# Self-attention of a decoder layer on one Trainium2 core: values as the stationary operand, four column tiles, and two stage borders in another order

## The chip, the cores and the metric

The kernel runs on one core of one Trainium2 chip. The metric is the device time of that core in microseconds (us), the median of several runs. TensorE is called PE here (its weight loads PEld), VectorE DVE, ScalarE ACT, GpSimd POOL and SyncE, which issues all the transfers, SP.

## The reference

One decoder layer on x of 8 sequences x 128 tokens x 512 channels, float32: causal self-attention (32 heads of 16 channels, ALiBi bias), cross-attention to a context (32 query heads over 8 key/value heads of 128 channels, rotary embedding), and a feed-forward block, each followed by a residual add and a layer normalisation. The part that matters here:

```python
scores = einsum('bqhd,bkhd->bhqk', q, k) / sqrt(16) + alibi   # causal, h = 32 heads
attn = softmax(scores, axis=-1)
out = einsum('bhqk,bkhd->bqhd', attn, v).reshape(B, S, D)
x = layernorm(x + out @ w_out.T + b_out)
```

## The kernel before

Matmuls in the kernel run on "split" operands: a float32 value is written as a high part in the reduced format fp32r and a low part (value minus high part), and a product is three matmuls (high x high, high x low, low x high: `product`, L34). ACT makes the high part by a copy, DVE or POOL the low part by a subtraction.

There are four stages, each with a method for every engine, and every engine works through its own list in order, held back by semaphores alone. **A** (`ProjectSelf`) computes q, k and v of self-attention: 16 tiles of q and k, which go through DRAM into the layout of the heads, and 8 tiles of v, one for each sequence, and splits the context on the side. Each tile goes from PE to `A_val` (DVE), is split by ACT and POOL, and the values end in `vhl` (16 high, then 16 low channels for every head). **B** (`AttendSelf`) is the self-attention, 64 steps n = 8b + G: sequence b, group G of 4 heads. **C** is the cross-attention (64 steps) and **D** the feed-forward block.

In a step n of B, PE (`tensor`) issues the scores of group n (2 matmuls, L777), the product of probabilities and values of group n-4 (`weigh`, L748 and L749), the transposes of the probabilities of group n-2 (L789), then half a tile (6 matmuls) of the cross-attention's keys and values (`project`), which fill PE while the softmax is on the way. Twice in eight steps 6 matmuls of the output projection come ahead of that (`close`). DVE (`minima`, L825) adds the mask, writes the negated scores to `prob` (3 slots) and takes their minimum; ACT takes the exponentials in place with their sum (L676); the transposed probabilities are split by ACT (L659) and DVE (L833). In `weigh` the 128x128 transposed probabilities of one head are the stationary operand and the head's 32 or 16 value columns are moving, so the output has queries on partitions. ACT (L668) and DVE (L840) add the two halves, POOL divides 16 heads at a time by their sums (`scale`, L595), PE transposes the result (L797), ACT and DVE split it (L690, L845).

The cross-attention's keys and values share the engines. With four steps to a pair of tiles, n = 0 mod 4 has the last of both: ACT, behind the exponentials of step n, makes the high part of a value tile (L683) and of a key tile (L695); DVE the low part of the value tile (L895); POOL, first thing in its step n, the low part of the key tile (L615, waits for L695). POOL adds the rotated halves at n = 3 mod 4 (L627). POOL also has the low parts of the weights (L166), the inverse root (L108) and the normalisation of a row (L113).

At the border of A and B the context's last pieces and the first weights of B come through `stage`, a ring of five slots that A uses with three more of its own. A loads the pieces, then B's first five pieces, each as soon as its slot is free; B's first weight piece (`B_wk`) takes slot 0, which holds one of A's last. At the border of B and C, seven more steps (`STEPS` = 71) take the last groups through; the tables `QUERY`, `ROTATE` and `NEXT_SPLIT` spread the first four query tiles of C (`cross.project`, `cross.rotate`) over them. C's step 1 is the first that begins with `scores`, since scores(0) is issued in B.

Of the kernel before, what the change touches and what calls it, by code (L numbers as in the profile page):

```python
# [23 lines left out]
KV = 4 * NT  # L24

# [113 lines left out]
class Ring:  # L139
# [9 lines left out]

    def load(self, eng, n, src):  # L150

        wait(eng, self.s_lo, n - self.SLOTS + 1)
        dst = self.stage[:, n % self.SLOTS, :]
        if len(src.shape) == 3:
            dst = dst.rearrange("p (g n) -> p g n", g=src.shape[1])
        eng.dma_start(dst, src).then_inc(self.s_piece[n % self.SLOTS], 16)

    def hi(self, eng, n, out):

        eng.wait_ge(self.s_piece[n % self.SLOTS], 16 * (n // self.SLOTS + 1))  # L160
        eng.activation(out, self.stage[:, n % self.SLOTS, :], ACT.Copy).then_inc(self.s_hi, 1)  # L161

    def lo(self, eng, n, hi, out):

        eng.wait_ge(self.s_hi, n + 1)
        eng.tensor_tensor(out, self.stage[:, n % self.SLOTS, :], hi.bitcast(F32), ALU.subtract).then_inc(self.s_lo, 1)  # L166
# [49 lines left out]
class ProjectSelf:  # L216

    RING = 8  # L220
# [13 lines left out]
    def __init__(self, chip, stage, cT, vhl, heads, ident, power, trig, dram):  # L234
        sem = lambda name: chip.sem("A_" + name)
        self.stage, self.cT, self.vhl, self.heads, self.ident, self.power, self.trig = stage, cT, vhl, heads, ident, power, trig
# [15 lines left out]
        self.s_val, self.s_vhi, self.s_vlo = sem("val"), sem("vhi"), sem("vlo")  # L252
# [22 lines left out]
    def sync(self, eng, ring, sources):  # L275
# [28 lines left out]
        for n in range(self.CONTEXT + C, len(self.pieces)):  # L304
            self.load_piece(eng, n)
        heads.load(eng, 0, 1)
        for n in range(Ring.SLOTS):
            eng.wait_ge(self.s_lo, max(j for j in range(len(self.pieces)) if j % self.RING == n) + 1)
            ring.load(eng, n, sources[n])
# [11 lines left out]
    def scalar_tile(self, eng, i):  # L321

        kind, m, h = self.order[i]
        if kind == "qk":
            for n in self.pieces_with(i):
                self.piece_hi(eng, n)
        eng.wait_ge(self.s_val, i + 1)
        src = self.val[:, i % 2, :]
        if kind == "qk":
            if i >= self.heads.RING:  # L330
                eng.wait_ge(self.heads.s_store[i % self.heads.RING], 16 * (i // self.heads.RING))
            dst = self.tiles[i % self.heads.RING][:, 0, :]
        else:
            dst = self.vhl[:, m, :, 0:DH]
            src = src.rearrange("p (h d) -> p h d", d=DH)
        eng.activation(dst, src, ACT.Copy).then_inc(self.s_vhi, 1)
        if kind == "v":
            for n in self.pieces_with(i):
                self.piece_hi(eng, n)
# [42 lines left out]

    def vector_tile(self, eng, i):
# [6 lines left out]
        wait(eng, self.s_vlo, i - 1)  # L390
# [3 lines left out]
        if kind == "v":  # L394
            eng.tensor_tensor(out, acc, self.bv[:, :], ALU.add).then_inc(self.s_val, 1)  # L395
# [15 lines left out]
    def gpsimd_tile(self, eng, i):  # L411

        kind, m, h = self.order[i]
        eng.wait_ge(self.s_vhi, i + 1)
        src = self.val[:, i % 2, :]
        if kind == "qk":
            hi, lo = (self.tiles[i % self.heads.RING][:, j, :] for j in range(2))
        else:
            src = src.rearrange("p (h d) -> p h d", d=DH)
            hi, lo = self.vhl[:, m, :, 0:DH], self.vhl[:, m, :, DH:2 * DH]  # L420
        eng.tensor_tensor(lo, src, hi.bitcast(F32), ALU.subtract).then_inc(self.s_vlo, 1)

    def gpsimd(self, eng):
# [12 lines left out]
        for i in range(len(self.order)):  # L436
            self.gpsimd_tile(eng, i)
            if i == 0:
                eng.wait_ge(self.s_ident, 32)
                eng.tensor_scalar(self.trig[:, 0:2, :], self.trig[:, 0:2, :], -1.0, None, ALU.mult)\  # L440
                   .then_inc(heads.s_causal, 1)


class AttendSelf:

# [13 lines left out]

    NEXT_LOAD = {57: range(5), 62: (5, 6), 64: (7,), 67: (8,)}  # L460
    NEXT_SPLIT = {60: (0,), 61: (1,), 62: (2,), 65: (3,), 70: (4, 5, 6, 7)}
    QUERY = {64: 0, 65: 1, 66: 2, 67: 3}
# [460 lines left out]
class AttendCross:  # L923
# [248 lines left out]
    def vector(self, eng, n):  # L1172
# [5 lines left out]
        if n == 0:  # L1178
            self.minima(eng, n)
# [601 lines left out]
```

## Time and profile before

| what | value |
|---|---|
| median of 3 runs | 954.91 us (952.61 to 955.36) |
| the profiled execution | 952.4 us, its span 950.6 us |
| busy in the span | PE 901.9, PEld 765.9, DVE 673.7, ACT 498.4, POOL 522.3 us |
| mean granted PE clock | 0.989 of full speed |

The span runs from the first to the last instruction on the core. "Busy" of PE counts matmuls whose modelled spans overlap, so what a matmul costs is the distance to the start of the next. A view by stretches gives the busy time of each engine with the number of its instructions, and the granted clock (1.00 is 2.4 GHz, 0.50 is 1.2 GHz). A timeline row is: start, length, engine, line, instruction, tiles, shape, count, and in brackets the engine's idle time ahead of it with what ended it.

### The profile page before, as it was taken

What the parts mean: (1) busy time and instruction counts of PE and PEld (TensorE: products, weight loads), DVE (VectorE), ACT (ScalarE), POOL (GpSimd) and SP (SyncE); (2) the same over time, 40 slices, a digit from 0 to 9 for tenths busy, and PEclk for the clock granted to TensorE, in tenths of its full rate; (3) what the DMA queues carried; (4) which work ended last, traced back from release to release, by engine and by line L of the source; (5) the groups of instructions that cost most, each with busy time, mean ns of one, the idle gap of its engine ahead of it and who ended that gap; (6) DMA issues with size and microseconds to landing.
All of it is one profiled execution on the core that took longest, in us unless ns stands there. A gap on an engine that the chain in (4) does not pass through costs nothing.

```text
span 950.6 us, 15757 instructions
## 1 busy us (share of the span) xinstructions
PE 901.9 (95%) x4812; PEld 765.9 (81%) x4812; DVE 673.7 (71%) x2166; ACT 498.4 (52%) x1565; POOL 522.3 (55%) x443
## 2 busy tenths in 40 slices
PE   7996999999999789999999999999999999999996
PEld 6785988888888668888888888888888887787884
DVE  5465767777777658777777777777777777655646
ACT  4335877776777245455555455555445566340320
POOL 4544843353234566666666666666666678654001
PEclk9998999999999989999999999999999999999999
DMA  7688986576544611131131311313113113010000
GB/s 273 257 204 189 248 178 121 141 162 122 134 122 157 254 56 34 42 125 34 34 122 34 126 42 34 123 34 116 41 44 123 34 56 109 15 34 23 23 12 33
DMA packets 68371, 96.65 MB, mean 102 GB/s; under 512 B 7232, under 2 KB 44352, under 8 KB 67264
## 3 DMA queue, kind: packets, MB, share of 16 engines
q1 hardware_dynamic: 68288, 95.65, 34.7%
q8 instruction: 39, 0.64, 0.3%
q14 instruction: 44, 0.36, 0.2%
HBM read 68.33 MB, written 27.26 MB: 101 GB/s over the span
## 4 chain that ended last, share of the span: by engine, by line
PE 79%; ACT 6%; issue 6%; DVE 6%; POOL 2%; DMA 0%; POOLq 0%; ACTq 0%; DVEq 0%
PE banks L34 61%; PE banks L1102 4%; PE banks L1082 3%; PE banks L789 3%; PE banks L749 2%; ACT B_prob L676 2%; PE banks L748 2%; PE banks L1103 2%; PE banks L777 1%; POOL x L1620 1%; PE banks L121 1%; ACT C_prob L1032 1%; DVE A_val L395 1%; ACT cT L319 0%; DVE B_prob L825 0%
## 5 line engine op out<-in xcount | busy, mean ns | idle before, releaser
L34 PE MATMUL banks<-C_wo,C_o 128*128 128x512 f32 x768 | 190.3, 396 | 2.2 <-DVE C_o L1195 1.0
L34 PE MATMUL banks<-xT,C_w 128*128 128x512 f32 x768 | 186.9, 393 | 1.5 <-DVE xT L136 1.5
L34 PEld LDWEIGHTS banks<-xT,C_w 128*128 128x128 f32 x768 | 145.0, 190 | 32.0 <-issue 1.9
L34 PEld LDWEIGHTS banks<-C_wo,C_o 128*128 128x128 f32 x768 | 139.5, 188 | 30.5 <-issue 2.3
L1023 ACT ACTIVATE C_q<-C_t 128x512 fp32r<-128x512 f32 x64 | 40.5, 632 | 170.2 <-POOL C_t L1208 170.2
L676 ACT ACTIVATE B_prob<-B_prob,B_top 128x128 f32<-128x128 f32 x256 | 99.5, 391 | 33.2 <-DVE B_top L825 32.4
L1216 POOL TENSOR_TENSOR C_q<-C_t,C_q 128x512 fp32r<-128x512 f32 x64 | 82.9, 1295 | 47.6 <-ACT C_q L1023 47.6
L1032 ACT ACTIVATE C_prob<-C_prob,C_top 128x128 f32<-128x128 f32 x256 | 98.9, 389 | 0.3 <-DVE C_top L1166 0.3
L1208 POOL TENSOR_TENSOR C_t<-C_t,C_t 128x512 f32<-128x512 f32 x64 | 83.1, 1298 | 5.7 <-DVE C_t L1147 5.7
L1102 PE MATMUL banks<-C_kv,C_q 128*128 128x256 f32 x256 | 68.2, 344 | 5.0 <-issue 4.8
L166 POOL TENSOR_TENSOR C_wo<-stage,C_wo 128x512 fp32r<-128x512 f32 x32 | 41.0, 1284 | 57.8 <-ACT C_wo L161 57.8
L166 POOL TENSOR_TENSOR C_w<-stage,C_w 128x512 fp32r<-128x512 f32 x32 | 41.1, 1284 | 56.5 <-ACT C_w L161 56.5
L1224 POOL TENSOR_TENSOR C_prob<-C_prob,C_rden 128x512 f32<-128x512 f32 x64 | 66.5, 1040 | 2.2 <-DVE C_rden L1177 2.1
L825 DVE CUSTOM_DVE_ANT_0 B_prob<-banks,causal 128x128 f32<-128x128 f32 x256 | 58.9, 286 | 10.1 <-issue 9.8
L1049 ACT ACTIVATE C_o<-banks 128x512 fp32r<-128x512 f32 x64 | 38.3, 598 | 50.2 <-PE banks L34 50.2
L1195 DVE TENSOR_TENSOR C_o<-banks,C_o 128x512 fp32r<-128x512 f32 x64 | 44.2, 691 | 25.7 <-ACT C_o L1049 25.6
L1145 DVE TENSOR_TENSOR C_t<-banks,trig 128x512 f32<-128x512 f32 x64 | 44.2, 690 | 25.5 <-PE banks L34 25.5
L1166 DVE CUSTOM_DVE_ANT_0 C_prob<-banks,C_prob 128x128 f32<-128x128 f32 x256 | 58.9, 286 | 2.7
L34 PE MATMUL banks<-cT,B_wk 128*128 128x512 f32 x192 | 52.4, 409 | 7.9 <-POOL B_wk L166 7.7
L749 PE MATMUL banks<-vhl,B_pT 128*128 128x16 f32 x256 | 59.2, 256 | 0.0
L833 DVE TENSOR_TENSOR B_pT<-banks,B_pT 128x512 fp32r<-128x512 f32 x64 | 44.1, 689 | 20.4 <-ACT B_pT L659 20.2
L34 PE MATMUL banks<-C_pT,C_kv 128*128 128x512 f32 x192 | 54.3, 391 | 4.2 <-DVE C_pT L1184 2.1
(156 smaller groups left out, 2132.1 us busy)
## 6 DMA issues: line engine op xcount, KB each, us to landing
C_kv<-cross_kv_d SPq DMA_DIRECT2D x8, 2048.0 KB, 8.9
cross_kv_d<-B_k_out SPq DMA_DIRECT2D x16, 512.0 KB, 3.0
cross_kv_d<-B_v_out SPq DMA_DIRECT2D x16, 512.0 KB, 4.8
stage<-wq_dram SPq DMA_DIRECT2D x32, 256.0 KB, 2.6
stage<-wo_dram SPq DMA_DIRECT2D x32, 256.0 KB, 2.6
heads_q<-heads_q_d SPq DMA_DIRECT2D x96, 64.0 KB, 3.7
heads_k<-heads_k_d SPq DMA_DIRECT2D x96, 64.0 KB, 3.8
heads_q_d<-cT SPq DMA_DIRECT2D x8, 512.0 KB, 2.6
```

The lines of the kernel that those rows point to most:

```text
L34: mm = eng.matmul(out, stationary[i], moving[j], start=first and n == 0, stop=last and n == len(PASSES) - 1)
L166: eng.tensor_tensor(out, self.stage[:, n % self.SLOTS, :], hi.bitcast(F32), ALU.subtract).then_inc(self.s_lo, 1)
L676: last = eng.activation(e, e, ACT.Exp, bias=self.top[:, n % 4, h:h + 1], scale=-1.0, accum_out=self.total[:, HG * G + h:HG * G + h + 1])
L749: mm = eng.matmul(out[:, at:at + DH], self.pT[1][:, m % 2, h * S:(h + 1) * S], v[:, 0:DH], start=False, stop=True)
L825: last = eng.tensor_tensor_reduce(self.prob[:, n % 3, h * S:(h + 1) * S], self.sc[n % 2][:, h * S:(h + 1) * S], self.heads.causal, 1.0, 3e ...
L1032: last = eng.activation(e, e, ACT.Exp, bias=self.top[:, n % 2, h:h + 1], scale=-1.0, accum_out=self.total[:, n % 2, h:h + 1])
L1102: eng.matmul(out, q[0][:, h, tok], both, start=True, stop=False)
L1145: eng.tensor_tensor(by_batch(t1), by_batch(bank), cos, ALU.mult).then_inc(self.s_cos, 1)
L1166: last = eng.tensor_tensor_reduce(self.prob[:, n % 2, h * S:(h + 1) * S], self.sc[:, h // 2, h % 2, 0, :], self.prob[:, n % 2, h * S:(h + ...
L1208: eng.tensor_tensor(t1, t1, t2, ALU.add).then_inc(self.s_sum, 1)
L1216: eng.tensor_tensor(self.query(r, 1), by_batch(self.t1[:, r % 2, :]), self.query(r, 0).bitcast(F32), ALU.subtract).then_inc(self.s_qlo, 1)
L1224: eng.tensor_tensor(e, e, self.rden[:, (n - 1) % 2, :].unsqueeze(2).broadcast_to([P, self.Q, S]), ALU.mult).then_inc(self.s_norm, 1)
```

## The change

The values stay in full precision (`v`, float32, not split): for two heads the columns lie as v, 16 zeros, v, so that the 32 columns [v | 0] belong to the first head and [0 | v] to the second. `weigh` takes them as the stationary operand, with the transposed probabilities (float32, not split either, 128 columns) moving; two groups (8 heads) are done at once, four pairs of heads in the four column tiles of the array (output partitions 32q to 32q+31), 8 matmuls in every second step. The output is thereby already transposed, with channels on partitions. The division by the sums therefore moves ahead of the transposes, to all of the probabilities: `inverse` on DVE, `norm` on POOL, in every step. ACT's copy of the transposed probabilities stays (`copy_turned`); DVE's subtraction L833, the addition L668 and L840, `scale`, and the transposes L797 go. The row's normalisation moves from POOL to DVE, and `prob` has 4 slots. In A the value tiles are no longer split, POOL clears the zero columns, and `B_wk` takes the ring's slot that comes free first. At the end of B the last steps are written out in another order, the same in kind for all engines. In C, `scores(0)` moves to C's step 0, behind its two query tiles. Cut to its core (where a removed line is left out, it is in the functions above):

```diff
+VW = 3 * DH * HS // 2
...
+    def slot(self, n):                      # Ring
+        return (n + self.SLOTS - 1) % self.SLOTS
...
         heads.load(eng, 0, 0)               # ProjectSelf.sync
+        for n in range(Ring.SLOTS):
+            eng.wait_ge(self.s_lo, max(j for j in range(len(self.pieces)) if j % self.RING == ring.slot(n)) + 1)
+            ring.load(eng, n, sources[n])
+            if n == 0:
+                for j in range(self.CONTEXT + C, len(self.pieces)):
+                    self.load_piece(eng, j)
         heads.load(eng, 0, 1)
...
+        for n in self.pieces_with(i):       # scalar_tile
+            self.piece_hi(eng, n)
+        if i < self.QK:
+            eng.wait_ge(self.s_val, i + 1)
...
-        wait(eng, self.s_vlo, i - 1)        # vector_tile
+        wait(eng, self.s_vlo, min(i - 1, self.QK))
...
+            eng.tensor_tensor(self.values_of(self.v[:, m, 0:VW], 3)[:, :, 0:3:2, :], self.values_of(acc, 2),
+                              self.values_of(self.bv[:, :], 2), ALU.add).then_inc(self.s_val, 1)
...
+        for i in range(self.QK):            # ProjectSelf.gpsimd
             self.gpsimd_tile(eng, i)
...
+            if i == 1:
+                for b in range(B):
+                    last = eng.memset(self.values_of(self.v[:, b, 0:VW], 3)[:, :, 1, :], 0.0)
+                last.then_inc(self.s_pad, 1)
...
+    OT, CLOSE, ROW, ROOT, NORMAL, TURN, TAKE = 11, (12, 13), 14, 15, 16, 17, 18
...
+    def norm(self, eng, m):
+        eng.wait_ge(self.s_rden, m + 1)
+        e = self.prob[:, m % 4, :].rearrange("p (h s) -> p h s", h=HG)
+        eng.tensor_tensor(e, e, self.rden[:, m % 2, :].unsqueeze(2).broadcast_to([P, HG, S]), ALU.mult).then_inc(self.s_norm, 1)
...
     def gpsimd(self, eng, n):
         j = self.tile("k", n, 2)
         if j is not None:
+            self.key_lo(eng, j)
+        if n > 0:
+            self.norm(eng, n - 1)
...
+    def gpsimd_end(self, eng):
+        self.norm(eng, self.NS - 1)
+        self.key_lo(eng, len(self.FILL) // 2 - 1)
+        for i in range(3, 7):
             self.cross.piece_lo(eng, i)
...
     def scalar(self, eng, n):
+        if n >= self.LT:
+            self.copy_turned(eng, n - self.LT)
+        b = self.closing(n, self.TAKE)
         if b is not None:
             self.rows.hi(eng, b)
+        b = self.closing(n, self.OT)
+        if b is not None:
+            self.output_hi(eng, b)
+        eng.wait_ge(self.s_top, n + 1)
+        wait(eng, self.s_rden, n - 1)
...
+            self.value_hi(eng, j)
         j = self.tile("k", n, 2)
         if j is not None:
+            self.key_hi(eng, j)
...
+    def transpose(self, eng, m):
+        eng.wait_ge(self.s_norm, m + 1)
+        wait(eng, self.s_turned, m)
...
+    def weigh(self, eng, k):
+        b, c = k // C, k % C
+        eng.wait_ge(self.s_turned, 2 * k + 2)
...
+        for second in range(2):
+            for q in range(HG):
+                head = 2 * q + second
+                at = VW // HS * 2 * (4 * c + q) + DH * second
+                mm = eng.matmul(self.ov[b % 2][32 * q:32 * q + 32, c * S:(c + 1) * S], self.v[:, b, at:at + 2 * DH],
+                                self.pT[:, (2 * k + head // HG) % 4, head % HG * S:(head % HG + 1) * S],
+                                start=second == 0, stop=second == 1)
...
     def tensor(self, eng, n):
+        self.scores(eng, n)
+        if n >= self.LV and n % 2 == 0:
+            self.weigh(eng, (n - self.LV) // 2)
+        if n >= self.LT:
+            self.transpose(eng, n - self.LT)
...
+    def tensor_end(self, eng):
+        self.weigh(eng, (self.NS - self.LV) // 2)
+        self.transpose(eng, self.NS - 2)
+        self.cross.project(eng, 0)
+        self.cross.project(eng, 1, (0, 1))
+        self.transpose(eng, self.NS - 1)
+        self.turn(eng, B - 2)
+        self.cross.project(eng, 1, (2, 3))
+        self.weigh(eng, self.NS // 2 - 1)
+        self.cross.project(eng, 2, (0, 1))
+        self.close(eng, B - 1, range(C))
+        self.cross.project(eng, 2, (2, 3))
+        self.cross.project(eng, 3)
+        self.turn(eng, B - 1)
...
+    def inverse(self, eng, m):
+        eng.wait_ge(self.s_exp, m + 1)
+        wait(eng, self.s_norm, m - 1)
+        eng.reciprocal(self.rden[:, m % 2, :], self.total[:, m % 2, :]).then_inc(self.s_rden, 1)
...
     def vector(self, eng, n):
+        self.minima(eng, n)
+        if n > 0:
+            self.inverse(eng, n - 1)
...
             for n in range(c.STEPS):        # PE's list, stage C
                 d.tensor_ahead(eng, n)
+                if n < 3:
+                    c.queries(eng, n)
                 c.transpose(eng, n)
-                if n > 0:
-                    c.scores(eng, n)
+                c.scores(eng, n)
                 c.outputs(eng, n)
```

## Rows read from the trace of the kernel before

**Rows 1.** Stretches: length, busy (x) of PE, PEld, DVE, ACT, POOL; clock, DMA, GB/s.

```profile
90.00:325.00 235.00, 225.06 (x1453) 199.21 (x1452) 176.07 (x765) 173.04 (x645) 109.44 (x94) 1.00 0.67 167
75.50:83.00 7.50, 0.00 (x0) 0.00 (x0) 4.88 (x14) 2.97 (x6) 4.12 (x3) 0.76 0.69 128
83.20:86.00 2.80, 2.77 (x7) 2.25 (x8) 0.00 (x0) 2.34 (x10) 0.90 (x1) 0.50 0.95 249
325.96:330.75 4.79, 0.00 (x1) 0.03 (x1) 1.89 (x5) 0.76 (x2) 3.84 (x4) 0.77 0.16 68
```

**Rows 2.** PE's timeline, one step of B, and the same place eight steps later.

```profile
265.03 0.40 PE L777 MATMUL banks<-heads_k,heads_q 128*128 128x256 f32 x2
265.26 0.18 PE L748 MATMUL banks<-vhl,B_pT 128*128 128x32 f32 x1
...
266.08 0.66 PE L789 MATMUL banks<-ident,B_prob 128*128 128x128 f32 x4
266.49 1.63 PE L34 MATMUL banks<-cT,B_wk 128*128 128x512 f32 x6
267.95 0.40 PE L777 MATMUL banks<-heads_k,heads_q 128*128 128x256 f32 x2
...
293.81 0.40 PE L777 MATMUL banks<-heads_k,heads_q 128*128 128x256 f32 x2
```

**Rows 3.** Groups of instructions in 90:325, by shape: busy us, mean ns, idle before.

```profile
L748 PE MATMUL banks<-vhl,B_pT 128*128 128x32 f32 x256 | 54.4, 242 | 0.0
...
L659 ACT ACTIVATE B_pT<-banks 128x512 fp32r<-128x512 f32 x64 | 37.6, 588 | 21.3 <-PE banks L789 21.1
...
L797 PE MATMUL banks<-ident,B_o 128*128 128x128 f32 x32 | 4.9, 274 | 0.0
```

**Rows 4.** DVE's, ACT's and POOL's timelines in one step with a value and a key tile.

```profile
263.37 0.29 DVE L825 CUSTOM_DVE_ANT_0 B_prob<-banks,causal 128x128 f32<-128x128 f32 x1
...
264.22 0.69 DVE L833 TENSOR_TENSOR B_pT<-banks,B_pT 128x512 fp32r<-128x512 f32 x1
...
264.34 0.41 ACT L676 ACTIVATE B_prob<-B_prob,B_top 128x128 f32<-128x128 f32 x1 [0.70 <-DVE B_top L825]
...
265.90 0.57 ACT L683 ACTIVATE B_v_out<-banks 128x512 fp32r<-128x512 f32 x1
...
267.07 1.30 POOL L615 TENSOR_TENSOR B_k_out<-B_t,B_k_out 128x512 fp32r<-128x512 f32 x1 [0.97 <-ACT B_k_out L695]
```

**Rows 5.** The page's costliest groups, stage C: the same multiplication as `norm`.

```profile
L1224 POOL TENSOR_TENSOR C_prob<-C_prob,C_rden 128x512 f32<-128x512 f32 x64 | 66.5, 1040 | 2.2 <-DVE C_rden L1177 2.1
```

**Rows 6.** PE's, DVE's and POOL's timelines at the border of A and B.

```profile
0.75 1.80 POOL L428 MEMSET heads_k<- 128x2048 f32 x1
...
75.10 0.40 PE L777 MATMUL banks<-heads_k,heads_q 128*128 128x256 f32 x2
83.23 2.90 PE L34 MATMUL banks<-cT,B_wk 128*128 128x512 f32 x6 [7.73 <-POOL B_wk L166]
85.92 0.54 PE L777 MATMUL banks<-heads_k,heads_q 128*128 128x256 f32 x2
...
81.89 0.28 DVE L825 CUSTOM_DVE_ANT_0 B_prob<-banks,causal 128x128 f32<-128x128 f32 x1
...
81.37 1.72 POOL L166 TENSOR_TENSOR B_wk<-stage,B_wk 128x512 fp32r<-128x512 f32 x1
```

**Rows 7.** PE's timeline at the border of B and C.

```profile
300.12 0.40 PE L777 MATMUL banks<-heads_k,heads_q 128*128 128x256 f32 x2
...
308.14 2.88 PE L34 MATMUL banks<-xT,C_w 128*128 128x512 f32 x12
...
330.75 0.55 PE L1102 MATMUL banks<-C_kv,C_q 128*128 128x256 f32 x1 [4.79 <-issue]
...
335.06 7.44 PE L34 MATMUL banks<-xT,C_w 128*128 128x512 f32 x24 [1.50 <-DVE xT L136]
...
363.56 0.36 PE L1102 MATMUL banks<-C_kv,C_q 128*128 128x256 f32 x1
```

More of the change, by code:

```diff
@@ L411, in gpsimd_tile @@
     def gpsimd_tile(self, eng, i):
-        kind, m, h = self.order[i]
         eng.wait_ge(self.s_vhi, i + 1)
[L415 to L421, printed above, removed]
+        hi, lo = (self.tiles[i % self.heads.RING][:, j, :] for j in range(2))
+        eng.tensor_tensor(lo, self.val[:, i % 2, :], hi.bitcast(F32), ALU.subtract).then_inc(self.s_vlo, 1)
     def gpsimd(self, eng):
@@ L670, in scalar @@
-        if self.live(n):
-            eng.wait_ge(self.s_top, n + 1)
-            if G % 4 == 0:
-                wait(eng, self.s_rden, n // 4 - 1)
-            for h in range(HG):
-                e = self.prob[:, n % 3, h * S:(h + 1) * S]
-                last = eng.activation(e, e, ACT.Exp, bias=self.top[:, n % 4, h:h + 1], scale=-1.0,
-                                      accum_out=self.total[:, HG * G + h:HG * G + h + 1])
-            last.then_inc(self.s_exp, 1)
+        b = self.closing(n, self.OT)
@@ L679, in scalar @@
+        if b is not None:
+            self.output_hi(eng, b)
+        eng.wait_ge(self.s_top, n + 1)
+        wait(eng, self.s_rden, n - 1)
+        for h in range(HG):
+            e = self.prob[:, n % 4, h * S:(h + 1) * S]
+            last = eng.activation(e, e, ACT.Exp, bias=self.top[:, n % 4, h:h + 1], scale=-1.0,
+                                  accum_out=self.total[:, n % 2, h:h + 1])
+        last.then_inc(self.s_exp, 1)
         j = self.tile("v", n, 0)
         if j is not None:
-            eng.wait_ge(self.s_pj, self.FILL.index(("v", j)) + 1)
@@ L757, in close @@
             eng.wait_ge(self.s_olo, b + 1)
+            wait(eng, self.s_z, b)
+            wait(eng, self.rows.s_lo, b)
             if b == 0:
@@ L791, in tensor @@
-        b = self.closing(n, 14, (62, 67))
-        if b is not None:
-            eng.wait_ge(self.s_o, 2 * b + 2)
-            wait(eng, self.s_z, b)
-            wait(eng, self.rows.s_lo, b)
-            for c in range(C):
-                mm = eng.transpose(self.ot[:, c * P:(c + 1) * P], self.o[:, 8 * c:8 * c + 8, :].rearrange("p h d -> p (h d)"),
-                                   self.before.ident)
-            mm.then_inc(self.s_ot, 1)
-        b = self.closing(n, 20, (65, 69))
-        if b is not None:
-            if b == B - 1:
-                self.cross.scores(eng, 0)
-            eng.wait_ge(self.s_z, b + 1)
-            self.rows.transpose(eng, b)
@@ L857, in vector @@
     def vector(self, eng, n):
[L859 to L864 removed]
+        self.minima(eng, n)
+        if n > 0:
+            self.inverse(eng, n - 1)
+        b = self.closing(n, self.NORMAL)
+        if b is not None:
+            self.rows.normalise(eng, b)
+        b = self.closing(n, self.TAKE)
         if b is not None:
             self.rows.lo(eng, b)
[L867 to L876 removed]
+        b = self.closing(n, self.OT)
         if b is not None:
```

378 lines of the change are left out of this document (150 added, 228 removed).

## The prediction

> **What bounds the kernel now.** I first read the stretches. In 90:325, the self-attention, PE is busy 225 of 235 us at full clock, with ACT at 173 (74%), DVE at 176 and POOL at 109 [rows 1]. The reader should see a stage that looks bound by PE, but whose second engine in the order of the softmax, ACT, is not far off. Then PE's timeline, since busy spans of matmuls overlap: from one scores to the next a step without extras takes 2.92 us (265.03 to 267.95): 0.23 scores, 0.82 to 0.9 for `weigh`, 0.41 transposes, 1.46 for six products [rows 2]. Eight steps take 28.78 (265.03 to 293.81), 3.6 each [rows 2], since the closing products and some waits come on top. From the second scores to the last B takes 300.12 - 85.92 = 214.2 us [rows 6, 7]. Last, both borders: PE stands 7.73 us for `B_wk` [rows 6], and 4.79 and 1.50 us at the start of C [rows 7].
>
> **The change, part by part.**
>
> *Weigh.* Before: 8 matmuls a step in about 0.89 us (0.111 each, little above 0.82 between two start times [rows 2]), 256 of either kind [rows 3]; 1.78 for two steps. After: 8 for two steps, of 128 moving columns in full precision. No row has that. A product of 512 columns costs 1.46 / 6 = 0.24, so 128 columns 0.06 a pass [rows 2]; full precision is three passes wherever this kernel makes it by splitting. Eight one after the other: 1.44 us; four side by side: 0.36; and if each pass costs a weight load at the present 0.111, 2.7. I take 0.8 us a pair, between the first two, because loads and changes of the tiles come on top. PE then does 64 x 0.89 - 32 x 0.8 = 31 us less, and 8 x 0.36 = 3 less for the transposes L797 [rows 3].
>
> The Trainium skill ("FP8 and Floating Point Precision", TensorE Precision Notes) has true float32 at four passes: 1.92 us in a row, 0.48 side by side; no row here shows it. Against the change speaks "TensorEngine Tiling (Array Packing)", Key Properties: a change of the tiling mode drains the array, here twice a pair; no row shows that either. Both stay inside the bounds above.
>
> *What leaves DVE, what comes to POOL.* DVE loses L833 (0.62 a step from start to start, of 0.69 [rows 4]) and gains a reciprocal of four numbers. POOL loses `scale` and six normalisations, and gains `norm`, 1.04 us in each of 64 steps [rows 5]: 66 us, which POOL has, by sum.
>
> *The order decides, not the sum.* The chain of one group was scores, minima, exponentials, transposes; now inverse and `norm` stand ahead of the transposes, and the distance is still two steps. `norm` of n-1 is in POOL's step n, and the transposes that want it are in PE's step n+1. But at n = 0 mod 4 POOL's step n begins with `key_lo`, which waits for ACT's `key_hi`, and that is behind the exponentials and the value tile of the same step n. Before, that POOL wait held nobody: only stores and the next rotation were behind it.
>
> I wrote the queues of the 64 steps out in their order, each instruction starting when its engine is free and its semaphores are up. Durations: scores 0.23 (seen by DVE after 0.42), transposes 0.41 (by ACT after 0.68), six products 1.39, closing products twice 1.38 in eight steps [rows 2]; minima 0.92, exponentials 1.55 (264.34 to 265.90), value and key tile on ACT 0.50 and 0.53, DVE subtraction 0.62, POOL's 1.3 [rows 4]; ACT's copy 0.5 [rows 3]. For the kernel before this gives 211.2 us from the second scores to the last; the trace has 214.2. So the method is 1.4% short. For the kernel after, with steps 40 to 44 and scores(40) at 0:
>
> - ACT: copy of 38 at 2.62, exponentials(40) 3.12 to 4.67, value tile, key tile to 5.70 (DVE was late with minima(40), 1.3 to 2.3).
> - POOL: `key_lo` 5.82 to 7.12, only then norm(39) to 8.16, though its sums were there from 2.4.
> - PE: scores(41) at 3.74, then it wants the transposes of 39 and stands 4.24 us, to 8.21. scores(42) comes at 10.39, since the products of step 41 are behind.
> - ACT: copy of 39 at 8.89, exponentials(41) at 9.39, though their minima were ready at 6.8.
> - Steps 42 and 43 run at 2.8 and 2.0 us; scores(44) at 15.25, and it begins again (3.73 us of waiting there).
>
> A pair of cycles takes 31.8 us for eight steps against 28.4 by the same arithmetic before. Over the stage it is 250.7 against 211.2; scaled by 214.2 / 211.2, 254.2: **+40 us**. With a pair at 0.2 us it is 243.3, at 1.8 it is 265.0, at 2.8 it is 290.9: PE's saving is no longer on the path, a stall takes its place. What is late next if `norm` came ahead of `key_lo`: nothing as large, 206.4 us.
>
> *The clock.* PE stood 7.5 us from 75.5 with a mean clock of 0.76, so (0.76 - 0.5) / 0.5 x 7.5 = 3.9 us at full and the rest at half; in the 4.79 us the mean is 0.77, so 2.6 us at full [rows 1]. Then six products took 2.69 us (83.23 to 85.92) at 0.50 [rows 1, 6], 1.2 more. Stalls of 3.7 and 4.2 lie between. With 1.4 us more for the products behind each of the 15 stalls the arithmetic gives 268.7, so +18; with none 0. I take half: **+9**.
>
> *Border of A and B.* The value tiles no longer pass ACT and POOL; `B_wk` has the slot that is free from about 58 us, so its split does not end at 83.1 (81.37 + 1.72) [rows 6] but long before PE gets there. PE goes on from scores(0) at 75.10 [rows 6], instead of standing 7.73. But DVE has one more context piece behind the last value tile, so minima(0) come at about 77.4, not 81.89 [rows 6], and B's start runs as if scores(1) stood at 78.8 instead of 85.92: **-7** (bounds -4, minima alone, and -9). Loads of B's first four value pieces and of the second half of the heads move behind each other on SP; they are due four steps in, and the wait of the first steps covers them; at no cover they cost some 2. The eight clearings on POOL: 1.80 us for 2048 columns [rows 6], so 0.23 each, 1.8 us together, behind POOL's second tile, where PE has four banks ahead: 0, at most 1.8.
>
> *Border of B and C.* The last four weighings become two (-2), L797 leaves twice (-0.7). Following the list `tensor_end`: q0, q1 and half of q2 cover the last softmax (a wait of some 2.7 us for the close, because the high part of sequence 7 stands behind ACT's `tile_hi(0)` and four weight pieces), then q2's rest and q3, 4.1 us, cover the row, its root and its normalisation; PE then waits some 2.3 us for the last `lo`. From the last scores to C's scores(4) the trace has 363.56 - 300.12 = 63.4 us [rows 7]; I come to about 50, with 12 products at 2.76 [rows 7]. The idle 4.79 and 1.50 and the low clock after them, where 24 products took 7.44 instead of 5.7 [rows 7], go for the most part. I take **-12** (bounds -6 and -16), a bit less than worked out, as waits move more easily than they go. C's 60 other steps and D are as before.
>
> **Sum.** +40 + 9 - 7 - 12 = +30. The profiled execution is 952.4 us, so 982; the median of the runs, 954.9, lies 2.5 above it, so **985**.
>
> **The rivals.**
> 1. *The stall doesn't bind.* POOL's wait at `key_lo` is short or caught up, and `norm` is in time. For it: POOL has 109 of 235 us busy, DVE gets 40 us of room [rows 1, 3]. Against: ACT's order is fixed, and the key tile stands behind the exponentials (267.07 POOL starts 2.7 us after the exponentials do [rows 4]). It decides from the point at which `norm` ends before PE reaches the transposes, 4.2 us earlier than I have it. Then B takes 206.4 x 1.014 = 209.3: -5 - 7 - 12 = 931. Chance 0.12.
> 2. *PE stays the bound* and its savings count in full: -31 - 3 - 7 - 12, 902. Against it is ACT at 2.5 us a step. Chance 0.04.
> 3. *The column tiles don't run side by side*, so the change doesn't do what it says: 1.8 us a pair, +14 on the stage: 999. Chance 0.13; with weight loads at every pass (2.7 us, some +37) 1022, chance 0.04.
> 4. *The stall is there, but small*, and the borders pay for it: 950 to 960, 0.07.
> My forecast has 0.60.
>
> **The numbers.** The forecast's own range is 964 (no loss of clock, cheap pairs, borders at their best) to 1000 (clock lost after each stall, borders at half). The range is 948 to 1015: it leaves out rivals 1 and 2 and the dearest tiles. Faster by over 0.3%, which is about what a measurement of this kernel can tell from no change: rivals 1 and 2 and a part of 4, 0.18; same 0.03; slower 0.79.
>
> **What would show it.** PE's rows in B: a wait of about 4 us ahead of L789's successor in every fourth step, put down to `norm` on POOL; POOL's rows: `key_lo` starting behind ACT's key tile, with `norm` right behind it; eight steps at 31 to 33 us; the clock below 1.00 in the stretch of B; 8 matmuls of a pair within 0.4 to 1.5 us; no 7.7 us wait ahead of the first products of B. If eight steps take under 28 us, the order argument is wrong; if pairs take over 1.5, the tiles are.

## The result, and the profile after

The changed kernel takes 1001.5 us (median of 4 runs, 1000.52 to 1002.16) against 953.76 for the kernel before on the same chip: a ratio of 1.0502 [1.0474, 1.053], 5% slower. The profiled execution has a span of 1000.2 us against 950.6, 49.6 more; the forecast was +30 and 985 us.

Stretches of the kernel after: in the first row B but for its first steps, in the second eight of its steps (length; busy us and count of PE, PEld, DVE, ACT, POOL; clock, DMA, GB/s).

```profile
85.00:355.00 270.00, 202.38 (x1311) 162.67 (x1311) 127.54 (x705) 157.94 (x600) 134.39 (x122) 0.87 0.58 130
246.28:280.91 34.63, 25.81 (x177) 21.06 (x176) 17.67 (x95) 20.55 (x79) 15.00 (x14) 0.90 0.48 107
```

PE was busy 96% of B at a clock of 1.00 [rows 1]; now it is 75% at 0.87. No engine is nearly full: ACT 58%, POOL 50%. Eight steps take 34.63 us against 28.78 [rows 2]. PE's timeline in them, cut; the first step is one with n = 2 mod 4:

```profile
246.28 0.40 PE L755 MATMUL banks<-heads_k,heads_q 128*128 128x256 f32 x2
246.60 0.65 PE L781 MATMUL banks<-B_pT,v 128*32 128x128 f32 x16
247.18 0.66 PE L764 MATMUL banks<-ident,B_prob 128*128 128x128 f32 x4
...
254.82 0.40 PE L755 MATMUL banks<-heads_k,heads_q 128*128 128x256 f32 x2
259.17 1.11 PE L764 MATMUL banks<-ident,B_prob 128*128 128x128 f32 x4 [3.95 <-POOL B_prob L582]
260.08 1.06 PE L122 MATMUL banks<-ident,x 128*128 128x128 f32 x4
260.79 2.24 PE L35 MATMUL banks<-cT,B_wk 128*128 128x512 f32 x6
262.87 0.40 PE L755 MATMUL banks<-heads_k,heads_q 128*128 128x256 f32 x2
...
276.34 1.11 PE L764 MATMUL banks<-ident,B_prob 128*128 128x128 f32 x4 [3.70 <-POOL B_prob L582]
...
280.91 0.40 PE L755 MATMUL banks<-heads_k,heads_q 128*128 128x256 f32 x2
```

A pair of weighings (L781; 8 matmuls, each with two records) takes 0.58 us, 246.60 to 247.18. Then, in every fourth step, PE stands some 4 us ahead of the transposes of the group two back (L764), and what follows runs longer: the four transposes 1.11 us instead of 0.66, six products 2.24 instead of 1.63. The granted clock is 0.95 in the stall (254.82 to 259.17) and 0.60 from there to the next scores (259.17 to 262.87). The same time on POOL and ACT:

```profile
256.85 1.26 POOL L588 TENSOR_TENSOR B_k_out<-B_t,B_k_out 128x512 fp32r<-128x512 f32 x1 [2.19 <-ACT B_k_out L670]
258.07 2.04 POOL L582 TENSOR_TENSOR B_prob<-B_prob,B_rden 128x512 f32<-128x512 f32 x2
```

```profile
255.67 0.58 ACT L664 ACTIVATE B_v_out<-banks 128x512 fp32r<-128x512 f32 x1
256.15 0.62 ACT L670 ACTIVATE B_k_out<-B_t 128x512 fp32r<-128x512 f32 x1
260.32 0.60 ACT L650 ACTIVATE B_pT<-banks 128x512 f32<-128x512 f32 x1 [3.54 <-PE banks L764]
```

POOL stands 2.19 us for the high part of the key tile, makes the low part (`key_lo`, L588), and only then runs `norm` (L582), twice: the first of the two is a group late. PE waits for it, ACT waits 3.54 us for PE, and the exponentials of the next group stand behind ACT's copy. That is the ring of waits that the forecast wrote out. The view of waits over 85:355 (total us, times, longest):

```profile
ACT B_pT L650 <- PE banks L764: 102.0, 40, 3.8
...
PE banks L764 <- POOL B_prob L582: 67.6, 30, 4.2
POOL B_k_out L588 <- ACT B_k_out L670: 32.5, 15, 2.4
```

The last row, 15 waits of about 2.2 us, is the forecast's cause. The other two are PE and ACT waiting for each other and for POOL round the ring; the first experiment, which takes `norm` out of that wait, shrinks them.

The border of A and B, PE's timeline. Here the 7.73 us for `B_wk` [rows 6] are gone (0.54 is left), scores(1) begin at 76.75 instead of 85.92, and at once the stall and the low clock are there (0.50 from 82.54 to 86.02): `norm` of the first group was behind the low parts (`piece_lo`, L171) of two value weight pieces on POOL, 78.99 to 81.44 (second fence). Scores(8) begin at 105.38, in the kernel before at 105.32: the first eight steps gave all of it back.

```profile
75.30 1.61 PE L35 MATMUL banks<-cT,B_wk 128*128 128x512 f32 x6 [0.54 <-POOL B_wk L171]
76.75 0.40 PE L755 MATMUL banks<-heads_k,heads_q 128*128 128x256 f32 x2
...
82.54 1.11 PE L764 MATMUL banks<-ident,B_prob 128*128 128x128 f32 x4 [3.78 <-POOL B_prob L582]
83.31 2.91 PE L35 MATMUL banks<-B_wv,cT 128*128 128x512 f32 x6
```

```profile
78.99 2.50 POOL L171 TENSOR_TENSOR B_wv<-stage,B_wv 128x512 fp32r<-128x512 f32 x2 [3.84 <-ACT B_wv L166]
81.44 1.04 POOL L582 TENSOR_TENSOR B_prob<-B_prob,B_rden 128x512 f32<-128x512 f32 x1
```

The border of B and C, PE's timeline from the last scores (355.02) to C's scores(4):

```profile
372.00 5.46 PE L35 MATMUL banks<-B_wout,B_oT 128*128 128x512 f32 x12 [3.31 <-ACT B_oT L658]
...
383.91 5.73 PE L35 MATMUL banks<-xT,C_w 128*128 128x512 f32 x24 [1.50 <-DVE xT L137]
...
402.27 1.62 PE L35 MATMUL banks<-C_pT,C_kv 128*128 128x512 f32 x3 [3.44 <-DVE C_pT L1190]
...
413.00 0.36 PE L1108 MATMUL banks<-C_kv,C_q 128*128 128x256 f32 x1
```

58.0 us, against 63.4 [rows 7] and about 50 in the forecast. The idle 4.79 at C's start [rows 7] has gone, but 3.31 us stand ahead of the last close, with the clock at 0.50 in the 12 products behind them (372.00 to 377.26), 1.50 ahead of the second half's products, as before, and 3.44 ahead of C's first products of probabilities, where the kernel before waits 2.14:

```profile
352.93 0.93 PE L34 MATMUL banks<-C_pT,C_kv 128*128 128x512 f32 x3 [2.14 <-DVE C_pT L1184]
```

So the difference of the spans splits into: stage B from the second scores to the last 278.3 against 214.2 us (+64.1); its start 9.2 earlier; the end 5.4 shorter; together +49.5 of the 49.6. Of the 64.1, 9.2 fall in the first seven steps (28.6 us from scores(1) to scores(8), before 19.4) and 54.8 in the rest.

### The profile page after: what moved, and what is told of

Read it like the earlier page. It is cut to its first block, busy times and chain, and to the rows that moved or that the text cites. A ratio compares the mean times of both kernels' runs of the same rounds, so it can differ in the third digit from the quotient of the medians.

```text
span 1000.2 us, 15683 instructions
## 1 busy us (share of the span) xinstructions
PE 897.0 (90%) x4780; PEld 743.2 (74%) x4780; DVE 635.5 (64%) x2139; ACT 489.2 (49%) x1541; POOL 555.6 (56%) x486
## 4 chain that ended last, share of the span: by engine, by line
PE 70%; ACT 10%; POOL 10%; issue 5%; DVE 5%; DMA 0%; ACTq 0%; POOLq 0%; DVEq 0%
PE banks L35 56%; ACT B_prob L686 5%; PE banks L1108 4%; PE banks L764 3%; PE banks L1088 3%; POOL B_prob L582 3%; POOL B_k_out L588 2%; PE banks L1109 1%; PE banks L781 1%; POOL x L1625 1%; POOL B_wk L171 1%; ACT B_k_out L670 1%; ACT B_v_out L664 1%; PE banks L122 1%; POOL C_t L1213 1%
## 5 line engine op out<-in xcount | busy, mean ns | idle before, releaser
L764 PE MATMUL banks<-ident,B_prob 128*128 128x128 f32 x256 | 47.4, 314 | 72.5 <-POOL B_prob L582 72.5
L582 POOL TENSOR_TENSOR B_prob<-B_prob,B_rden 128x512 f32<-128x512 f32 x64 | 66.4, 1045 | 75.4 <-DVE B_rden L856 75.4
L764 PEld LDWEIGHTS banks<-ident,B_prob 128*128 128x128 f32 x256 | 31.4, 156 | 83.9 <-POOL B_prob L582 79.9
L650 ACT ACTIVATE B_pT<-banks 128x512 f32<-128x512 f32 x64 | 38.0, 594 | 105.0 <-PE banks L764 104.4
L171 POOL TENSOR_TENSOR C_w<-stage,C_w 128x512 fp32r<-128x512 f32 x32 | 41.1, 1285 | 55.4 <-ACT C_w L166 55.4
L171 POOL TENSOR_TENSOR C_wo<-stage,C_wo 128x512 fp32r<-128x512 f32 x32 | 41.1, 1287 | 54.3 <-ACT C_wo L166 54.3
L35 PE MATMUL banks<-cT,B_wk 128*128 128x512 f32 x192 | 63.9, 479 | 0.5 <-POOL B_wk L171 0.5
```

The source lines that it names most:

```text
L35: mm = eng.matmul(out, stationary[i], moving[j], start=first and n == 0, stop=last and n == len(PASSES) - 1)
L171: eng.tensor_tensor(out, self.stage[:, self.slot(n), :], hi.bitcast(F32), ALU.subtract).then_inc(self.s_lo, 1)
L582: eng.tensor_tensor(e, e, self.rden[:, m % 2, :].unsqueeze(2).broadcast_to([P, HG, S]), ALU.mult).then_inc(self.s_norm, 1)
L764: mm = eng.transpose(self.tp[:, h * S:(h + 1) * S], self.prob[:, m % 4, h * S:(h + 1) * S], self.before.ident)
```

## The experiments

All are edits of the changed kernel. e1 to e4 ran on one chip, where the kernel before took 953.05 us, e5 to e8 on one with 953.06, e9 and e10 on one with 952.64, the changed kernel itself on one with 953.76. Differences between kernels of different chips are therefore good to about 1 us. The matmuls added in e2, e9 and e10 write to a bank that nobody reads then; those of e3 and e8 compute the same output twice.

### Norm ahead of key_lo

```diff
     def gpsimd(self, eng, n):
         j = self.tile("k", n, 2)
-        if j is not None:
-            self.key_lo(eng, j)
         if n > 0:
             self.norm(eng, n - 1)
+        if j is not None:
+            self.key_lo(eng, j)
```

> The kernel after, with norm(n-1) ahead of key_lo in POOL's step. Theory (the stall comes from norm standing behind key_lo, which waits for ACT's key tile): the waits of about 4 us ahead of the transposes at n = 1 mod 4 go, eight steps take 26 to 28 us instead of 34.6, the clock in the self-attention is back at 0.98 or more, and the total falls by 50 to 65 us to 937 to 952 us, faster than the kernel before. Rival (norm in the chain two steps deep is too long whatever stands ahead of it): the stalls stay at 2 us or more, eight steps above 31 us, total above 975 us.

Measured: 933.01 us (931.82 to 933.36), 0.9792 [0.9777, 0.9806] of the kernel before. That is 68.5 us less than the change as made, a little more than the 50 to 65 expected, and 20 less than the kernel before. One stretch, the waits over 85:340 (which runs on past the last scores, at 285.21), and PE's and POOL's rows at the same point of the cycle:

```profile
120.00:285.00 165.00, 150.33 (x1118) 121.11 (x1119) 113.78 (x607) 133.84 (x511) 103.85 (x95) 0.99 0.70 157
```

```profile
ACT B_pT L650 <- PE banks L764: 27.3, 30, 2.6
PE banks L764 <- POOL B_prob L582: 23.6, 28, 2.5
```

```profile
240.04 0.40 PE L755 MATMUL banks<-heads_k,heads_q 128*128 128x256 f32 x2
241.11 0.66 PE L764 MATMUL banks<-ident,B_prob 128*128 128x128 f32 x4 [0.67 <-POOL B_prob L582]
...
243.43 0.40 PE L755 MATMUL banks<-heads_k,heads_q 128*128 128x256 f32 x2
```

```profile
239.83 1.23 POOL L582 TENSOR_TENSOR B_prob<-B_prob,B_rden 128x512 f32<-128x512 f32 x1
242.06 1.30 POOL L588 TENSOR_TENSOR B_k_out<-B_t,B_k_out 128x512 fp32r<-128x512 f32 x1 [1.00 <-ACT B_k_out L670]
```

POOL still waits for the key tile, but `norm` is ahead of it. PE's wait at this point is 0.67 us, the clock in the stretch 0.99, and eight steps take 25.07 us (240.04 to 265.11), where 26 to 28 were expected. From the second scores to the last it is 285.21 - 76.14 = 209.1 us; the queues written out ahead of the result gave 209.3 for this order. One position in one list of instructions is the whole loss, and more: against the kernel before, scores(8) are 2.6 us earlier, the last scores 14.9 and C's scores(4) 20.8.

### The stall filled, so that the clock stays

```diff
         self.scores(eng, n)
+        if n >= 5 and n % 4 == 1:
+            eng.wait_ge(self.s_top, n)
+            for _ in range(14):
+                eng.matmul(self.sc[(n + 1) % 2], self.cT[0][:, 0, 0:P], self.cT[0][:, 0, 0:D], start=True, stop=True)
```

> The kernel after, with 14 matmuls of 512 columns behind the scores of every step n = 1 mod 4 from 5 on; they write the free score bank, are overwritten by the next scores, and lie in the time in which PE stands (3.2 us of 3.7 to 4.2). Theory (half of the loss beyond the forecast is the clock, which falls after each stall): the granted clock of the self-attention goes from 0.87 to 0.97 or more, the products behind a stall take 1.4 us instead of 1.9 to 2.7, and the total falls by 12 to 25 us. Rival (the slow products are hidden by ACT's queue): less than 4 us change, though the clock is up.

Measured: 977.62 us (977.21 to 979.46), 1.0266 [1.0251, 1.0281]; 23.9 less than the change as made, at the top of what was expected. PE's rows:

```profile
231.68 0.40 PE L755 MATMUL banks<-heads_k,heads_q 128*128 128x256 f32 x2
...
256.52 3.36 PE L811 MATMUL banks<-cT 128*128 128x512 f32 x14
260.41 0.66 PE L764 MATMUL banks<-ident,B_prob 128*128 128x128 f32 x4 [0.53 <-POOL B_prob L582]
260.82 1.63 PE L35 MATMUL banks<-B_wout,B_oT 128*128 128x512 f32 x6
...
263.66 0.40 PE L755 MATMUL banks<-heads_k,heads_q 128*128 128x256 f32 x2
```

`norm` comes as late as before (from the scores at 256.28 to the transposes it is 4.13 us, in the change as made 4.10 and 4.35), but the transposes take 0.66 and the products 1.63, at a granted clock of 1.00 (260.41 to 263.66). Eight steps are 31.98 us (231.68 to 263.66); the forecast's arithmetic without any clock says 31.8. From the second scores to the last it is 253.7 us, for the forecast's 254.2 without the clock. So the 68.5 us between the change as made and e1 are 23.9 for the clock and 44.6 for the order; against the kernel before, the stage's 64.1 are 24 for the clock and 40 for the order.

### The weighings doubled, and in one column tile

```diff
-        for second in range(2):
+        for second in (0, 1, 0, 1):
```

> The kernel after, with each pair's 8 matmuls issued twice (the second pass starts the sums again, so the result is the same): 32 x 0.6 = 19 us more of PE work. Theory (PE is not the bound of the self-attention, but the scores of the next step wait behind the weighing at n = 2 mod 4 and 0 mod 4, partly on the path): 3 to 9 us more. Rival (PE's own work is the bound): 19 us more. Third case: under 2 us, all hidden in the stalls.

Measured: 1009.11 us (1008.15 to 1009.96), 1.0592 [1.0577, 1.0608]: +7.6, within the theory's range.

In the other kernel all eight matmuls go to column tile 0, and the other three tiles' output is missing:

```diff
-                mm = eng.matmul(self.ov[b % 2][32 * q:32 * q + 32, c * S:(c + 1) * S], self.v[:, b, at:at + 2 * DH],
+                mm = eng.matmul(self.ov[b % 2][0:32, c * S:(c + 1) * S], self.v[:, b, at:at + 2 * DH],
...
-                                start=second == 0, stop=second == 1)
+                                start=True, stop=True)
```

> The kernel after, with all 8 matmuls of a pair written to output partitions 0 to 31, so one column tile instead of four, and each started anew: the output of self-attention is left incomplete. Theory (the four tiles work side by side): a pair takes 1.5 to 2.0 us from the scores to the transposes instead of 0.6, and the total rises by 8 to 18 us. Rival (matmuls of 128 columns in full precision follow each other at the same distance in one tile as in four): a pair stays within 0.1 us of 0.6 and the total within 2 us.

Measured: 1026.08 us (1023.91 to 1027.49), 1.0765 [1.0743, 1.0786]: +24.6, more than the 8 to 18 expected. PE's rows, first of the doubled kernel, then of the one with one tile:

```profile
248.97 1.08 PE L781 MATMUL banks<-B_pT,v 128*32 128x128 f32 x32
249.98 0.66 PE L764 MATMUL banks<-ident,B_prob 128*128 128x128 f32 x4
```

```profile
247.12 1.93 PE L781 MATMUL banks<-B_pT,v 128*32 128x128 f32 x16
248.99 0.66 PE L764 MATMUL banks<-ident,B_prob 128*128 128x128 f32 x4
```

Sixteen matmuls in four tiles take 1.01 us, so eight more cost 0.43. Eight in one tile take 1.87, against 0.58 as the change has them: the tiles do run side by side, 3.2 times as fast, and the rival that they don't is out. With the 0.15 us that a pair costs beyond those 0.43 taken from both, it is 1.72 against 0.43, four times. At 128 moving columns one matmul in a row is 1.87 / 8 = 0.234 us, 3.8 times the 0.06 of a pass. The Trainium skill ("FP8 and Floating Point Precision", TensorE Precision Notes) has true float32 at four passes, and by that figure my estimates were 1.92 in a row and 0.48 side by side: the trace lies nearer these than the 1.44 and 0.36 of the three passes that I took from the split products. It doesn't count the passes: without the 0.15, one matmul is 0.215.

PE's work in the change as made is partly on the path. In e3, 32 x 0.43 = 14 us of it were added and 7.6 appear; in e4, 32 x 1.29 = 41 us and 24.6.

### The ring's order as before (with norm ahead)

```diff
     def slot(self, n):
-        return (n + self.SLOTS - 1) % self.SLOTS
+        return n % self.SLOTS
```

The loads on SP stand in their old order too (the context's rest and the second half of the heads first).

> The kernel with norm first (e1), and the ring and the order of the loads at the border of A and B as before the change (B_wk in slot 0, behind the context's last pieces and the second half of the heads). Theory (the first eight steps, not the start of B_wk, set how much the border gives: in e1 the ninth scores are only 2.6 us ahead of the kernel before): B_wk comes some 2 us later and the total rises by 0 to 4 us. Rival (the border is worth the 7 us of the forecast): 6 to 9 us more.

Measured: 939.01 us (933.6 to 940.05), 0.9845 [0.9819, 0.987]; the median is 6 us more than with the new order. The five runs scatter widely and one, at 933.6, took hardly longer than e1: by the intervals it is 2 to 8 us, so neither the expected 0 to 4 nor the rival's 6 to 9 is ruled out by the times. PE's rows in the profiled run (937.42 us, 5.6 more than e1's):

```profile
81.72 2.90 PE L35 MATMUL banks<-cT,B_wk 128*128 128x512 f32 x6 [5.98 <-POOL B_wk L171]
84.41 0.63 PE L754 MATMUL banks<-heads_k,heads_q 128*128 128x256 f32 x2
```

The wait for `B_wk` is back (5.98 us), with the low clock behind it (0.50 from 81.72 to 84.41). Scores(1) are 8.3 us later than in e1 (84.41 against 76.14), scores(8) 6.4, the last 5.6 (290.76 against 285.21). So in this run the border's gain lasts, once `norm` is in time: 5.6 us, near the rival. It is a gain over the old order in this kernel, though, not over the kernel before: from scores(1) to scores(8) the kernel before takes 19.4 us, e1 26.6 and e5 24.7, so e1 is only 2.6 us ahead of it at scores(8) and e5 3.8 behind.

### The last close earlier, and its gaps filled

```diff
-        self.cross.tile_hi(eng, 0)
         self.output_hi(eng, B - 1)
+        self.cross.tile_hi(eng, 0)
```

(ACT's list at the end of B, with norm ahead.)

> The kernel with norm first (e1), and at the end of B ACT makes the high part of sequence 7's output ahead of tile_hi(0) instead of behind it. Theory (PE's 3.3 us ahead of the last closing products are the wait for ACT, which stands behind four weight pieces on POOL): the wait shrinks to 1 us or less, the products behind it run at full clock, and the total falls by 2 to 5 us. Rival (what is won moves to the wait for the row or to C's query tiles): within 1 us.

Measured: 934.08 us (932.74 to 934.87), 0.9802 [0.9788, 0.9815]: nothing gained. PE's rows show why:

```profile
299.29 2.97 PE L35 MATMUL banks<-B_wout,B_oT 128*128 128x512 f32 x12
...
308.50 0.63 PE L122 MATMUL banks<-ident,x 128*128 128x128 f32 x4 [2.15 <-issue]
311.28 8.44 PE L35 MATMUL banks<-xT,C_w 128*128 128x512 f32 x24 [2.16 <-DVE xT L137]
319.56 0.28 PE L1108 MATMUL banks<-C_kv,C_q 128*128 128x256 f32 x1
```

In e1 the 12 products of the close came at 302.22, behind 3.32 us of waiting; here they come at 299.29, behind none, and at full clock: 2.81 us from start to start instead of 4.42. The products behind them begin 4.5 us earlier (302.10 against 306.64), though B's last scores were 0.5 us later (285.73 against 285.21). But the row that the close ends is late now: its inverse root on POOL begins at 307.26, behind the rotation and the low part of a query tile (304.01 to 307.31), and DVE waits for it (below). So PE waits 2.15 us and 2.16 us, where e1 has one wait of 1.50, and the 24 products behind take 8.44 us instead of 5.73. C's first scores are at 319.56, in e1 at 318.72. DVE's row:

```profile
307.85 0.55 DVE L114 TENSOR_SCALAR x<-x,first_moments,first_rstd 128x512 f32<-128x512 f32 x1 [3.72 <-POOL first_rstd L109]
```

The next kernel keeps that order and puts nine matmuls of 512 columns in each gap:

```diff
         self.cross.project(eng, 3)
+        self.fill(eng, self.NS, 9)
         self.turn(eng, B - 1)
+        self.fill(eng, self.NS, 9)
```

> The close of the last sequence stays ahead (as in e6_close_early), and in the two gaps that its trace shows before the first products of the second half of C (2.15 us ahead of the row's transposes at 308.50, 2.16 us behind them) PE gets nine matmuls of 512 columns each, of no use to the result, 2.2 us at full clock. Theory: the row and its root on POOL set when C goes on, so the gaps stay, but the clock doesn't fall in them, and the 24 products behind them take some 5.8 us instead of 8.44: 2.5 us less than 934.1, that is 931 to 932. Rival A: the products of C are not on the path there (the rotations on DVE and POOL are), so the time is within 0.7 us of 934.1. Rival B: the added matmuls are in the way of the row's transposes, 935 or more.

Measured: 931.28 us (930.31 to 931.84), 0.9775 [0.9762, 0.9789], 2.8 less than e6, as the theory said, and 1.7 less than e1. The rows:

```profile
306.04 2.20 PE L843 MATMUL banks<-B_oT 128*128 128x512 f32 x9
...
308.75 2.33 PE L843 MATMUL banks<-B_oT 128*128 128x512 f32 x9
311.16 5.70 PE L35 MATMUL banks<-xT,C_w 128*128 128x512 f32 x24
```

The row's transposes and the products start where they did, but the 24 products take 5.70 us and C's first scores come at 317.14 instead of 319.56: the low clock behind two gaps of 2.2 us (the granted clock is 0.65 from 311.28 to 319.70 in e6, 1.00 from 311.16 to 317.00 here) had cost 2.7. The gaps themselves stay. So the 5 us that the early close gained were eaten by both, 2.8 by longer waits for the row and 2.6 by the low clock behind them, and only the second part comes back.

### The first value pieces earlier

```diff
-    PIECES = (("k", 0, -1), ("v", 0, 0), ("v", 1, 0), ("v", 2, 1), ("v", 3, 1), ...
+    PIECES = (("k", 0, -1), ("v", 0, -1), ("v", 1, -1), ("v", 2, 0), ("v", 3, 1), ...
```

> The kernel with norm first (e1), and at the start of B the first two value weight pieces are split ahead of step 0 and the third in step 0, instead of two in step 0 and two in step 1. Theory (PE's 3.8 us ahead of the first transposes in B and the low clock after them are POOL doing the value pieces ahead of norm(0)): the wait falls to 2 us or less and the total by 2 to 5 us. Rival (the pieces come too late from DRAM, ACT and POOL stand for them instead): 0 to 3 us more.

Measured: 931.78 us (931.26 to 933.33), 0.9782 [0.9768, 0.9795]: 1.2 us less than e1, within what the runs scatter, and short of the 2 to 5 expected. The wait ahead of the first transposes is 3.30 us, not 2 or less: in e1 it was 4.15. The third piece, now in step 0, still stands ahead of `norm` on POOL (78.67 to 79.93, `norm` at 79.89), though the inverse sums were there at 78.28. The first transposes come at 80.98 instead of 82.31, the last scores 1.8 us earlier (283.43), C's scores(4) only 0.55 (342.23 against 342.78): most of it was lost at the end, 0.8 of it in the close's 12 products, which take 5.26 us here and 4.42 in e1, behind the same wait.

### The weighings doubled where the stage is mended

e1 and the doubling of e3 together.

> The kernel with norm first (e1), and each pair's matmuls issued twice, as in e3. Theory (without the stall PE's work is most of the path again): of the 32 x 0.5 = 16 us of added work 10 to 16 us appear, against 7.6 us in e3. Rival (ACT, busy 2.5 us a step, is the bound of the repaired stage): 5 us or less.

Measured: 937.59 us (937.11 to 938.03), 0.984 [0.9826, 0.9853]: +4.6 over e1, for 32 x 0.43 = 14 us more of work on PE. The number is the rival's: two thirds of the added work are hidden, so PE's own work is not the bound of the mended stage either. That ACT is the bound, as the rival has it, is not shown. In e1's stretch above ACT is 81% busy, PE 91% by spans that overlap; the softmax's chain sets part of the steps and PE part. Which of its links, no run here isolates.

### All together

```diff
+        if n == 2:                    # behind the scores
+            eng.wait_ge(self.s_top, 2)
+            for _ in range(10):
+                eng.matmul(self.sc[1], self.cT[0][:, 0, 0:P], self.cT[0][:, 0, 0:D], start=True, stop=True)
```

with the edits of e1, e6, e7 and e9.

> Everything that helped, in one kernel: norm ahead of key_lo, the first value pieces early (e7_values_early, 3.30 us of waiting ahead of the first transposes at 80.98), ten matmuls of no use in that wait, the last close early and its two gaps filled (as in e9_tail_filled). Theory: the first six products of B's value tile take 1.6 us instead of 2.79 with the clock held, and what e7 and e9 gain adds to it: 1.2 us below e7 for the start, and 2.5 for the end if e9 has them, so 927.5 to 930. Rival: what the start gains is given back in the stage, as in e7, where 1.8 us at the last scores were 0.5 in the span; then 929.5 to 932.

Measured: 930.23 us (928.94 to 931.09), 0.9764 [0.9749, 0.9778], the fastest, though its interval overlaps that of e9. It lies just above the theory's 927.5 to 930, in the rival's range. PE's row at the start, behind the wait:

```profile
82.85 1.64 PE L35 MATMUL banks<-B_wv,cT 128*128 128x512 f32 x6
```

The clock is held (1.00 from 82.44 to 84.32; six products in 1.64 us, where the change as made has 2.91), and scores(3) are at 84.32 instead of e9's 86.07. By scores(8) 0.6 us of that is left (102.43 against 103.00): PE waits 0.89 and 0.82 us for `B_wk` and the heads' loads, and a later wait of 2.77 us, ahead of 93.60, has the low clock behind it (0.54 to 96.89). Against e7, which has the same early pieces and no added matmuls, nothing is left: its scores(8) are at 101.04.

## Why the prediction was right, and where it was off

**The order (+40): right.** The stall stands where it was forecast, ahead of the transposes in every fourth step, and has its length: 3.95 and 3.70 us (259.17, 276.34) for 4.24 and 3.73. The steps fit one by one: from the scores of a step n = 0 mod 4 (251.12) the next come after 3.70 us (forecast 3.74), the ones after that after 11.75 (10.39, and 1.4 of clock), and then steps of 2.78 and 2.06 (2.8 and 2.0). e2, without the clock, has eight steps of 31.98 us for 31.8 and the stage of 253.7 for 254.2, and e1 the stage of 209.1 us for 209.3. The first rival, `norm` in time, describes e1 (its 931 us came out at 933), not the change; the second, PE as the bound with 902 us, describes no run.

Two things in it are less exact than the sum looks. The pair stood in the arithmetic at 0.8 us and measured 0.58; by the forecast's own figures (243.3 at 0.2, 250.7 at 0.8) that is 3 us less of stage, which something else made up for. And the sentence that PE's saving is "no longer on the path" doesn't agree with those figures, by which some 40% of it is, nor with e3 and e4, where 55 and 60% of the added work appear.

**The clock (+9): the term that was mis-sized.** It measured 24. With 1.4 us behind each of the 15 stalls the arithmetic gave +18, with none 0, and the forecast took half, as it left open whether the clock falls in stalls of 3.7 and 4.2 us. The rows show it low behind both that are printed above (0.60 from 259.17 to 262.87, 0.55 from 276.34 to 279.53). From the transposes to the next scores PE takes 3.70 us (259.17 to 262.87), in e1, at the same place of the cycle, 2.32 (241.11 to 243.43), so 1.4 us is lost, as the forecast had it; over the stage e2 puts it at 23.9 / 15 = 1.6 us a stall. It is paid in full, presumably because what PE issues late is what ACT's next exponentials, and so the next `norm`, wait for. So the +18 was the better choice, and still 6 short.

**The border of A and B (-7): right in kind, but not collected.** Scores(1) came 9.2 us earlier, a little beyond the bound of 9, and scores(8) 0.1 later. The first steps have the same fault, `norm` behind another low part on POOL, here `piece_lo`: the forecast's list of durations has none for POOL's weight pieces, and only the `key_lo` stall is written out. With `norm` ahead of `key_lo`, e5 against e1 gives 6 us by the medians, with the scatter said above; against the kernel before only 2.6 us are left at scores(8), even in e1.

**The border of B and C (-12): mis-sized, 5.4.** It stands below the lower bound of 6. The waits for the close (3.31 for 2.7) and for the last low part (1.50 for 2.3) were near. The failing step is the listing of the waits up to C's scores(4): the close's 12 products took 372.00 to 377.26, 5.3 us, where 2.8 were put in (299.29 to 302.10 in e6, with no wait ahead), since the clock fell in the wait ahead of them, and C's first products of probabilities wait 3.44 us, where the trace of before had 2.14.

**The pair of weighings (0.8 us): 0.58,** within the bounds, made of 0.43 for eight matmuls side by side and 0.15 once a pair. In one column tile it is 1.87, above the 1.44 taken from three passes. Against this change the Trainium skill ("TensorEngine Tiling (Array Packing)", Key Properties) has the array drained at each change of the tiling mode; if the 0.15 are that, and the scores to weighing distance of 0.32 instead of 0.24, it is 0.23 us a pair, 7 us of PE's work in all; no run isolates the drain.

**The sum.** From the second scores to the last it is 64.1 us, 24 of them the clock (for 9) and 40 the order (for 40); the start is 9.2 (for 7), the end 5.4 (for 12): 49.5 for 30. That the total is still inside the range is in part luck. The measured 1001.5 us lie just above the forecast's own range of 964 to 1000, whose upper end has the clock lost and the borders at half; the range went on to 1015 to take in dearer tiles, and these did not come. The time is also next to the 999 of the third rival, tiles that don't run side by side, which e4 rules out: only the rows and e1, e2 and e4 tell the two apart.

## What to carry to other kernels

When an operation is moved onto the path of a software pipeline, write out the list of the engine that gets it and ask what the instruction just ahead of it waits for: a sum of busy times (POOL had half its time free) says nothing of it, and swapping two neighbours was worth 68 us here. Count what PE does behind a stall at the lower clock with the stall itself, all the more where it is in a cycle. And when one wait at a border is removed, name the next one before the gain is booked: here the early close's 5 us came back as 2.8 us of longer waits and 2.6 us of low clock.

## What the runs showed of the hardware

Full-precision matmuls with 32 stationary and 128 moving columns run side by side in four column tiles: eight in 0.58 us, in one tile 1.87, and eight more in four tiles 0.43. The granted clock fell in stalls of 3.7 to 4.2 us (0.60 and 0.55 behind those at 259.17 and 276.34), and in e6 with two gaps of 2.15 and 2.16 us close together (1.00 up to 308.50, 0.82 from there to 311.28, 0.65 behind): six products behind a stall took up to 2.91 us instead of 1.63, and 24 products behind the gaps 8.44 instead of 5.73. The length of a wait alone doesn't tell: behind 1.88 us in e1 the clock was 0.64 (93.86 to 96.64), behind 1.81 at the same place in e9 1.00 (94.15 to 96.04). Matmuls of no use in the gaps kept it up (e2 0.987 over the span, the change as made 0.955). The result's next work began when it did without them: the transposes 4.13 us after the scores in e2 (4.10 and 4.35 in the change as made), the row's transposes at 308.37 in e9 (308.50 in e6). They bought 23.9 us in e2 and 2.8 in e9.
